# Softmax attention on Trainium2: one summed exponential tile a head in place of two

## What is computed

```python
scores = jnp.einsum('bqhd,bkhd->bhqk', q, k) * scale
weights = jax.nn.softmax(scores, axis=-1)
out = jnp.einsum('bhqk,bkhd->bqhd', weights, v).reshape(B, Lq, D)
return out @ w_o + b_o
```

## Time and profile before

| | |
|---|---|
| runs | 1731.08 us median, 1725.13 to 1731.60 |
| span of the profiled execution | 1727.3 us (its own time is not listed beside the three runs) |
| softmax attention | about 650 to 1438 us of the span |
| TensorE busy | 1589.8 us (92%), 8932 matmuls |
| VectorE busy | 1226.5 us (71%) |
| ScalarE busy | 1150.9 us (67%) |
| GpSimd busy | 1022.9 us (59%) |
| mean granted TensorE clock | 0.975 of full speed |

### The profile page before, as it was taken

How to read it: one execution, slowest core, us unless ns; L and a number is a source line. 1 busy time by engine, 2 the same in 40 slices (tenths; PEclk the granted TensorE clock), 3 DMA queues, 4 the chain that set the end, 5 groups by cost and what they waited for, 6 DMA issues and landing times. The chain is left out here.

```text
span 1727.3 us, 29488 instructions
## 1 busy us (share of the span) xinstructions
PE 1589.8 (92%) x8932; PEld 719.8 (42%) x8932; DVE 1226.5 (71%) x1756; ACT 1150.9 (67%) x1895; POOL 1022.9 (59%) x738
## 2 busy tenths in 40 slices
PE   5999878998999977899999999999999978999998
PEld 3545433443444432334444444444443423444443
DVE  4978898997888745676776767676767665665553
ACT  5667599787888744665757666666657567556662
POOL 4776436765678723565657666665756665455452
PEclk9989999999999997999999999999999989999999
DMA  8421000000000122121211212121211200010001
GB/s 309 146 73 32 1 1 1 1 1 1 0 1 1 45 59 81 32 58 25 58 34 36 56 27 57 27 55 32 58 25 40 55 22 28 25 49 24 24 24 49
DMA packets 60463, 72.22 MB, mean 42 GB/s; under 512 B 14416, under 2 KB 40016, under 8 KB 59856
## 3 DMA queue, kind: packets, MB, share of 16 engines
q1 hardware_dynamic: 56944, 62.22, 12.3%
q10 hardware_dynamic: 3424, 8.91, 1.3%
HBM read 37.40 MB, written 8.39 MB: 27 GB/s over the span
## 5 line engine op out<-in xcount | busy, mean ns | idle before, releaser
L1556 DVE TENSOR_REDUCE s_mx<-bank 128x1 f32<-128x512 f32 x512 | 337.3, 685 | 199.8 <-PE bank L1684 193.7
L1443 ACT ACTIVATE s_E<-bank 128x512 f32<-128x512 f32 x512 | 293.9, 595 | 202.5 <-PE bank L1698 177.2
L1342 POOL TENSOR_TENSOR s_E<-s_E 128x1024 f32<-128x1024 f32 x128 | 300.5, 2367 | 125.4 <-PE bank L1706 117.9
L1684 PE MATMUL bank<-s_KA,s_QA 96*128 96x512 f16 x512 | 194.2, 390 | 17.7 <-DMA s_KA<-sm_cx 7.1
L1698 PE MATMUL bank<-s_QA,s_KA 97*128 97x512 f16 x512 | 196.7, 386 | 3.8 <-DMA s_QA<-s_mrow 1.4
L1335 POOL TENSOR_TENSOR sm_cx<-s_qkf,sm_cx 128x512 f16<-128x512 f32 x64 | 76.5, 1195 | 175.6 <-ACT sm_cx L1421 175.4
L1867 POOL TENSOR_TENSOR sm_cx<-m_xf,sm_cx 128x512 f16<-128x512 f32 x60 | 84.1, 1408 | 104.9 <-ACT sm_cx L1909 104.9
L1706 PE MATMUL bank<-s_E,s_V 128*32 128x512 f32 x1024 | 135.6, 602 | 4.3 <-ACT s_E L1443 4.3
L1075 PE MATMUL bank<-sm_zz,w1raw 128*128 128x512 f16 x256 | 100.3, 392 | 31.1 <-DVE sm_cx L962 16.3
L1098 PE MATMUL bank<-f_w2q,w2raw 128*128 128x512 f16 x512 | 122.2, 380 | 0.4 <-ACT w2raw L912 0.4
L772 POOL TENSOR_TENSOR sm_wkv<-sm_wkv,sm_cx 128x511 f32<-128x511 f32 x48 | 66.1, 1378 | 94.2 <-DVE sm_wkv L962 94.1
(11 more groups left out here) (264 smaller groups left out, 4092.1 us busy)
## 6 DMA issues: line engine op xcount, KB each, us to landing
sm_cx<-in_ctx SPq DMA_DIRECT2D x16, 768.0 KB, 4.6
s_QA<-sm_cx SPq DMA_DIRECT2D x384, 32.0 KB, 1.9
s_KA<-sm_cx SPq DMA_DIRECT2D x372, 32.0 KB, 1.9
X<-in_x SPq DMA_DIRECT2D x8, 1024.0 KB, 6.8
out_x<-X SPq DMA_DIRECT2D x8, 1024.0 KB, 4.3
w1raw<-in_w ACTq DMA_DIRECT2D x1, 4096.0 KB, 14.2
w2raw<-in_w ACTq DMA_DIRECT2D x1, 4096.0 KB, 28.7
w1raw<-in_wq SPq DMA_DIRECT2D x1, 1024.0 KB, 5.1
```

The source lines that it names most:

```text
L1342: e.tensor_tensor(into, into, other, ALU.add).then_inc(s_sum.sem, 1)
L1443: e.activation(E[:, SLOT[k] + h, :], SC[u % 2][:, :], ACT.Exp, scale=1.0 / float(np.sqrt(DH)))\
L1556: e.tensor_reduce(mx[:, q, h:h + 1], MX[q % 2][:, :], AX.X, ALU.max).then_inc(s_red.sem, 1)
L1684: e.matmul(MX[k % 2][:, :], QA[0:MROW, m, h, q * P:(q + 1) * P], KA[0:MROW, m, h, :], start=True, stop=True).then_inc(s_mx.sem, 1)
```

## The change

The sums of a group become one chain. `summed` takes k = 0, 1, 2 by a table `SUMMED`: tile 1 is added to tile 0 (slot 4 into 0), that sum into tile 2 (slot 0 into 8), and tile 3 into that (slot 4 into 8). Each is two instructions, so six a step in place of four. k = 0 and k = 1 stand where p = 0 and p = 1 stood, k = 2 stands in the next step, between `low` 0 and `low` 1 (after the last step, behind it). TensorE's `denominators` of p = 0 goes away; the one at unit 6 of the next step multiplies the single sum in slot 8 with ones. The waits of ScalarE's exponentials, VectorE's reciprocals and the tallies follow.

```diff
--- before.py
+++ after.py
@@ -1188,6 +1188,7 @@
     LATE_RC = {10: (0,), 14: (1, 2, 3)}
     RC_UNITS, AN_UNIT = ({14: (0, 1, 2, 3)}, {7: (0,), 9: (1,), 12: (2,), 13: (3,)}, LATE_RC, LATE_RC), 14
     SLOT = (0, 4, 8, 4)
+    SUMMED = ((0, 4), (8, 0), (8, 4))
     MAX_AHEAD = 2
     PV_UNIT, DN_LATE = (6, 10, 14), 6
     END_BANK, END_UNITS = (6, 7, 2, 3), (3, 5, 9, 12)
@@ -1233,7 +1234,7 @@
         s_mT, s_mrow = tally("mT", NG), tally("mrow", NG)
         s_md = [tally(f"md{m}", 1, 16) for m in range(NG)]
         s_sc, s_ex, s_pv = tally("sc", 16 * NG), tally("ex", 16 * NG), tally("pv", 16 * NG)
-        s_sum, s_dn, s_av = tally("sum", 4 * NG), tally("dn", 8 * NG), tally("av", NG)
+        s_sum, s_dn, s_av = tally("sum", 6 * NG), tally("dn", 4 * NG), tally("av", NG)
         s_rc, s_an = tally("rc", 4 * NG), tally("an", NG)
         s_ab, s_ah, s_al = (tally(n, NG) for n in ("ab", "ah", "al"))
         s_o, s_res, s_bo = tally("o", TT), tally("res", TT), tally("bo", TT)
@@ -1334,11 +1335,18 @@
                 s_qkh.wait(e, b, 2 * m + w + 1)
                 e.tensor_tensor(qkl[:, w, :], qkf[:, :], qkh[:, w, :], ALU.subtract).then_inc(s_qkl.sem, 1)
 
-            def summed(b, m, p, i):
-
-                into, other = (E[:, s + 2 * i:s + 2 * i + 2, :] for s in SLOT[2 * p:2 * p + 2])
-                s_pv.wait(e, b, 16 * m + 8 * p + 4)
-                s_ex.wait(e, b, 16 * m + 8 * p + 4 + 2 * i + 2)
+            def summed(b, m, k, i):
+
+                into, other = (E[:, s + 2 * i:s + 2 * i + 2, :] for s in SUMMED[k])
+                if k == 0:
+                    s_pv.wait(e, b, 16 * m + 4)
+                    s_ex.wait(e, b, 16 * m + 4 + 2 * i + 2)
+                if k == 1:
+                    s_pv.wait(e, b, 16 * m + 12)
+                    s_sum.wait(e, b, 6 * m + i + 1)
+                if k == 2:
+                    s_ex.wait(e, b, 16 * m + 12 + 2 * i + 2)
+                    s_sum.wait(e, b, 6 * m + 2 + i + 1)
                 e.tensor_tensor(into, into, other, ALU.add).then_inc(s_sum.sem, 1)
 
             def divided(b, m):
@@ -1359,6 +1367,10 @@
                     if m == 2:
                         context(b + 1)
                     low(*proj, 0)
+                if div:
+                    summed(*div, 2, 0)
+                    summed(*div, 2, 1)
+                if proj:
                     low(*proj, 1)
                 if last and m == 1:
                     s_p.wait(e, b, 2 * NG - 1)
@@ -1390,6 +1402,8 @@
             low(0, 1, 1)
             e.wait_ge(s_raw[3], 32)
             steps(step, e)
+            summed(B - 1, NG - 1, 2, 0)
+            summed(B - 1, NG - 1, 2, 1)
             mixed(2)
             mixed(3)
             for q in range(TT):
@@ -1430,14 +1444,14 @@
 
                 k, h = divmod(u, 4)
                 if k == 0:
-                    s_dn.wait(e, b, 8 * m - 4)
+                    s_sum.wait(e, b, 6 * m - 3 + h // 2)
                 if k == 1:
-                    s_sum.wait(e, b, 4 * m - 1 + h // 2)
+                    s_sum.wait(e, b, 6 * m - 1 + h // 2)
                     s_pv.wait(e, b, 16 * m)
                 if k == 2:
-                    s_dn.wait(e, b, 8 * m)
+                    s_dn.wait(e, b, 4 * m)
                 if k == 3:
-                    s_sum.wait(e, b, 4 * m + 1 + h // 2)
+                    s_sum.wait(e, b, 6 * m + 1 + h // 2)
                     s_pv.wait(e, b, 16 * m + 8)
                 e.wait_ge(s_sc.sem, s_sc.count(b, 16 * m + u + 1))
                 e.activation(E[:, SLOT[k] + h, :], SC[u % 2][:, :], ACT.Exp, scale=1.0 / float(np.sqrt(DH)))\
@@ -1556,7 +1570,7 @@
                 e.tensor_reduce(mx[:, q, h:h + 1], MX[q % 2][:, :], AX.X, ALU.max).then_inc(s_red.sem, 1)
 
             def reciprocals(b, m, i):
-                s_dn.wait(e, b, 8 * (m + 1))
+                s_dn.wait(e, b, 4 * (m + 1))
                 e.reciprocal(DEN[:, i * P:(i + 1) * P], DEN[:, i * P:(i + 1) * P]).then_inc(s_rc.sem, 1)
 
             def divide(b, m):
@@ -1706,12 +1720,11 @@
                     e.matmul(NUM[h * DH:(h + 1) * DH, :], V[:, m, t, h * DH:(h + 1) * DH], E[:, SLOT[t] + h, :],
                              start=(t == 0), stop=(t == TT - 1)).then_inc(s_pv.sem, 1)
 
-            def denominators(b, m, p):
-                if p == 0:
-                    s_an.wait(e, b, m)
-                e.wait_ge(s_sum.sem, s_sum.count(b, 4 * m + 2 * p + 2))
+            def denominators(b, m):
+                s_an.wait(e, b, m)
+                e.wait_ge(s_sum.sem, s_sum.count(b, 6 * (m + 1)))
                 for h in range(4):
-                    e.matmul(DEN[h * DH:(h + 1) * DH, :], ones[:, 0:DH], E[:, SLOT[2 * p] + h, :], start=(p == 0), stop=(p == 1))\
+                    e.matmul(DEN[h * DH:(h + 1) * DH, :], ones[:, 0:DH], E[:, SLOT[2] + h, :], start=True, stop=True)\
                         .then_inc(s_dn.sem, 1)
 
             def transposed(b, c, end=False):
@@ -1758,7 +1771,6 @@
                         maximum(*nxt, k)
                 if div:
                     attend(*div, TT - 1)
-                    denominators(*div, 0)
                 if m == 0 and nxt:
                     for k in range(MAX_AHEAD):
                         maximum(*nxt, k)
@@ -1778,7 +1790,7 @@
                     if proj and u in V_UNITS[m]:
                         values(*proj, V_UNITS[m].index(u))
                     if div and u == DN_LATE:
-                        denominators(*div, 1)
+                        denominators(*div)
                     if u in PV_UNIT:
                         attend(b, m, PV_UNIT.index(u))
                     if last and m == NG - 1 and u in END_UNITS:
@@ -1801,8 +1813,7 @@
             e.wait_ge(s_lo, 2)
             steps(step, e)
             attend(B - 1, NG - 1, TT - 1)
-            denominators(B - 1, NG - 1, 0)
-            denominators(B - 1, NG - 1, 1)
+            denominators(B - 1, NG - 1)
             for c in range(2, NG):
                 for q in range(TT):
                     output(B - 1, q, c, END_BANK[q], True)
```

## The result

The changed kernel takes 1759.42 us (median of 4 runs, 1755.53 to 1764.37) where the kernel before takes 1728.11 (with a fourth run of 1720.42): a ratio of 1.0208, interval 1.018 to 1.0235. The forecast was 1741 and the range ended at 1757. The direction was right, the size was not: +31 us for +10.

The account below looks back on a forecast made before the run. TensorE, busy 99.4 of 100 us in the attention stage, was taken as the bound. Batches +0.8, first batch's m=1 -0.9, tail +6.7 and clock +3.4 summed to +10.0 us: 1741 us, range 1728 to 1757.

Parts of the forecast that it names:

- the waits in m=2, m=3 and m=0: Denominators at unit 6: TensorE waits for GpSimd's last sum, stalling 1.24, 1.66 and 0.66 us in m=2, 3 and 0.
- the tail: End of the attention stage: the last sum has no next step to hide it, +6.7 us, bounds 0 and 10.
- the 0.9 of half clock: Last four denominators at the stage's end: taken at half clock after over 5 us of TensorE idling, 0.9 us more.
- the step on m=1: Step with the output projection: unit 6 comes late, so no stall on the last sum and the 0.86 us is kept.
- the clock: Half clock behind two of 14 new stalls in the attention batches: +3.4 us, bounds 0 and 24.
- cover: In m=1, the 2.3 us from the last sum's end (76.1) to TensorE's arrival (78.42), set against 1.1 us of contention.
- the sum would be the same: m=1: even if four normalisations cost 2.2 us by the skill's rule, not 1.1, that stays under the cover.
- the 14 new stalls: TensorE's waits for the last sum in m=2 and m=3, 1.24 and 1.66 us, 14 in all.
- the clock falls behind most stalls: Rival, new stalls in the attention batches: 14 x 1.7 = 24 us in place of 3.4, 1761 us; chance 0.10.
- The row-maximum transfer: Rival, DMA before the first score becomes the bound: about +1 us a batch, 1748 us; chance 0.12.
- in time: Rival, denominators at unit 6: GpSimd's last sum is never waited for, -20.8 us, 1710 us; chance 0.08.
- partial gain: Rival, batches or stage end: shorter hops or partly covered tail, -1 us a batch or -5 at the end, 1722 to 1734; 0.16.

Follow-up runs that it names:

- run 4: Changed kernel, m=1's last sum held until z is done, the last group's two pairs and two denominator groups restored, denominators at unit 7: 1734.84 us, ratio 1.0083.
- run 12: Changed kernel, but group 0 and the stage's last group keep two pairs and two denominator groups; denominators at unit 7 in m=2, 3, 0: 1712.8 us, ratio 0.9944.
- run 5: Changed kernel with the four normalised tiles z of m=1 made by ScalarE in place of VectorE: 1751.46 us, ratio 1.0165.
- run 1: Changed kernel with GpSimd's last sum at m=1 held back until VectorE's four normalisations are done: 1750.69 us, ratio 1.0172.
- run 2: Kernel before, only group 0's second pair of sums moved behind the first `low` of m=1, nothing added: 1744.54 us, ratio 1.0137.
- run 9: Changed kernel with the transposes of z in m=1 two units later (6, 8, 10, 12 for 4, 6, 8, 10): 1784.12 us, ratio 1.0347.
- run 7: Kernel before with only z made by ScalarE in place of VectorE: 1733.01 us, ratio 1.0060.
- run 10: Kernel before with only the transposes of z in m=1 two units later: 1742.5 us, ratio 1.0111.

## Why the prediction was right or wrong

**Right: the waits in m=2, m=3 and m=0.** Forecast +0.38, +0.80 and -0.20 us, measured +0.34, +0.77 and -0.21. The method, GpSimd's queue followed hop by hop, carried these. The three steps give back the gain as waits, and runs 4 and 12 confirm it the other way: with the wait taken away 0.9 us a batch of the gain is there, a third of the 2.6 us of three dropped groups.

**Right: the tail.** +6.7 us forecast. From the last transposes +6.3 were measured, but this length varies from trace to trace (40.9 us in run 12, 43.6 in the kernel before, which end alike), and the variation lies ahead of the middle sum: from its start it is 17.37 us in both. So the forecast is read from there. After, on GpSimd and TensorE:

```profile
1445.91 4.66 POOL L1350 TENSOR_TENSOR s_E<-s_E 128x1024 f32<-128x1024 f32 x2
...
1456.42 1.93 PE L1727 MATMUL bank<-s_E,ones 128*32 128x512 f32 x8 [8.84 <-POOL s_E L1350]
```

The denominators start 10.51 us after the middle sum for 4.72 before (1422.59 to 1427.31), 5.8 more as forecast, and take 1.93 us for 1.06 (the granted clock is 0.50 from 1455 to 1460), the 0.9 of half clock. To the next stage's first matmul it is 24.00 us for 17.37: +6.6.

**Wrong: the step on m=1.** "In m=1 the last sum now lies beside four normalisations on VectorE (0.54 us each). A `low` beside such an instruction took 1.44 us, one elsewhere 1.16, so 0.28 us for each, 1.1 us in all; the cover is 78.42 - 76.1 = 2.3 us, so nothing." The contention was seen, but charged to GpSimd alone and held against GpSimd's cover. The row used has VectorE's instruction start 0.12 us before GpSimd's, so that GpSimd is held; in the new place GpSimd starts first. With the `low` and additions of 2.35 us each already running it is VectorE that waits, by up to 1.4 us for one, and its cover was never worked out: z is due at unit 4, and after it come the reductions that TensorE waits for. Forecast for m=1: -0.86 us; measured +3.70. Over the eight steps m=1 that is 24.9 + 8 x 0.86 = 31.8 us, 3.4 of which stood in the sum as the clock's; the other 28.4 cover the whole miss of the stage with its tail in the two profiles (31.5 + 6.3 = 37.8 us for 10.0). Between the medians the growth is 31.3 us, and as wholes the two profiles differ by 28.0: the parts outside the stage took 9.8 us longer in the one of the kernel before.

The Trainium skill (SBUF — State Buffer, Who interferes with whom) had the rule: VectorE in a two-port mode, or with two inputs in SBUF, and GpSimd exclude each other for the whole instruction; the one that issues first has the ports and the other is fully blocked. The traces agree: 1.97 us for 0.54 behind the start of an addition, 1.11 for 0.15 behind that of a `low` in run 5, and GpSimd's 1.44 for 1.16 where VectorE starts first. The text read the rule as 2.2 us on GpSimd and said "the sum would be the same". It named the loser wrongly. With VectorE as the loser, z would have ended no earlier than the additions, 4.66 us for the pair, and in the kernel before the transposes start 0.3 us after the last z (1074.68 to 1074.99).

**Mis-sized: the clock.** Forecast: two of the 14 new stalls of 1.24 and 1.66 us, +3.4 us. The traces show none behind those stalls in the steady batches; the six stretches of reduced clock (10.2 us) all follow the wait for z in m=1 (2.79 to 2.85 us, 2.42 in the last), which was not in the list. The term was of the right kind, at the wrong place, and a third of the size. The rival "the clock falls behind most stalls" has nearly the measured time, 1761 us, but it is not what happened.

**Refuted: the other rivals.** The row-maximum transfer ends no step's wait in the steady batches of the changed kernel. The sums are not in time in m=2, 3 and 0, and there is no partial gain.

**What stays open.** Which stretches are followed by a reduced clock in runs 1, 2 and 5 (three to five of six batches, with nearly the same rows) was not settled. Why only 0.9 us a batch of the dropped denominators shows in runs 4 and 12 was not followed up.

## What to carry to other kernels

When an instruction moves to a new place in one engine's queue, price the contention for both partners, each against its own due time, and then for everything queued behind the one that is held; a busy share says nothing about it. Work out the gain of a change for each step of the loop: here the change in three groups of four, with the later unit and the old tail, gains 0.56% (0.3 to 0.8), and in all four it costs 2%. Look which of two instructions starts first: a normalisation and a `low` cost GpSimd 0.3 us in one order and VectorE 0.8 in the other. An experiment's own edit needs its control in the kernel before: runs 5 and 9 would have been misread without runs 7 and 10.

## What the runs showed of the hardware

- A VectorE instruction from SBUF to SBUF is held until 0.3 us after the end of the GpSimd instruction during which it starts: 1.97 us for 0.54, and for one of 128x4 elements, where there is nearly no data to move, 1.11 behind a `low` and 2.27 behind an addition for 0.15. All 28 normalisations of the changed kernel fit. Where VectorE starts 0.12 us earlier it keeps its 0.54 us and GpSimd's `low` takes 1.44 for 1.16 (kernel before). VectorE's reductions from PSUM beside the same additions keep their 0.68 us. GpSimd loses little while VectorE is held (5.02 us for two additions, for 4.66).
- ScalarE makes the same z in 0.81 us beside the same additions and beside none (805 and 806 ns on average): it takes no part in this.
- The wait for z of 2.79 to 2.85 us was followed by a reduced clock in every steady batch of the changed kernel, about 1.7 us lost each; waits of up to 1.06 us at the denominators (15 between 800 and 1300 us) were not, nor was the wait of 2.07 us at 786.24.
